# Interleaving the step-size products of one batch with the projections of the next on TensorE

## The chip, the core and the metric

The kernel runs on one core of a Trainium2 chip. The core has five engines that run their own instruction streams beside each other: TensorE (PE in the profile, with its weight loads shown as PEld), VectorE (DVE), ScalarE (ACT), GpSimd (POOL) and SyncE (SP), which here only issues DMAs. They wait for each other through counting semaphores; each engine works through its own stream in the order written. The metric is the time of one execution of the whole program in microseconds (us).

## The reference, cut to what matters

The program computes, for 8 batches of 512 tokens with 128 channels, `x + attn(layernorm(x)) + ffn(layernorm(x))`. The ffn is a mixture of 16 experts, 4 of them for each token. The attn part is a two-way Mamba block, which the change touches:

```
xz = einsum('ed,bld->bel', in_proj_w, hidden)            # 512 rows: x (256) and z (256)
for each direction (forward, backward):
    u      = silu(causal_conv(x) + conv_bias)            # 256 channels x 512 tokens
    x_dbl  = einsum('bdl,kd->bkl', u, xproj_w)           # 8 rows for the step size, 16 of B, 16 of C
    delta  = softplus(einsum('dr,brl->bdl', dtproj_w, x_dbl[:, :8]) + dt_bias)
    h      = scan(exp(delta * A), delta * B * u)         # 16 states for each channel
    y      = sum over states of h * C, + D * u, gated by silu(z)
```

"Projection" below is the product that gives x_dbl; "step-size products" are those with dtproj_w, whose output goes into delta.

## The kernel before, in words

The program has an opening (layer norm, routing, ranks), then the preparation of all 8 batches one after the other, then the main loop over the 8 batches (scans on VectorE, decays on ScalarE, products with C on GpSimd, sums and the ffn on TensorE). What a batch's preparation makes (delta, delta times u, the gate, the skip part, B and C) is stored to HBM, and the main loop reads it back.

The preparation works on whole batches: a batch has two directions (d = 0, 1) of two channel halves (h = 0, 1), 128 channels by 512 tokens each. It is pipelined over batches: while batch b goes through the step size, batch b+1 is projected, batch b+2 is convolved and batch b+3 is taken through the input projection.

On TensorE, `prepare(b)` (line 1170) issues in this order:

- the step-size products of batch b, direction 0 and then direction 1 (line 1176). Each direction has two products of 9 rows (8 rows of x_dbl and one of ones for the bias) by 128 by 512 in float32; each product shows as two matmul records, so a direction is four records. Direction d writes two PSUM banks from bank 4. It waits for `xd_sb` (ScalarE has copied x_dbl of this batch and direction) and for `delta_ready` of batch b-1 (VectorE has read the same banks).
- `project_u(b+1)` (lines 1155 to 1162): the projections of batch b+1, direction 0 and then 1, two products of 128 rows by 104 by 512 each, again four records for a direction. They write PSUM banks 2 and 3. They wait for `parts_ready` of batch b+1-1, that is for the ScalarE copy (line 915) that reads those two banks last, and for `u_ready` of their direction.
- the skip products (line 1185, eight records), `drop_part` (line 1167, which splits B and C into bfloat16 parts), `project_x(b+3)` (line 1145) and `project_z(b+3)` (line 1151).

On ScalarE, `prepare(b)` (lines 917 to 953) issues: a table load; for each direction the absolute value of the step-size products (line 923, waits for `dt_ps`) and its exponential (line 926); the logarithm of direction 0 (933); the copies of x_dbl of batch b+1, direction 0 (905 and 906, wait for `xd_ps`); the square of direction 0 (937, waits for VectorE's minimum); logarithm and square of direction 1; the x_dbl copies of direction 1; the copy of the skip products (943); the copies 910 and 887 (the latter waits for `project_x`); SiLU of batch b+2 (899); SiLU of z (892); and last the copy 915, which sets `parts_ready`.

On VectorE, `prepare(b)` (lines 1471 to 1505) issues: three of four taps of the convolution of batch b+2 (1459, 1464); the minimum of direction 0 and of direction 1 (1481, each waits for that direction's exponential, `exp_ready`); the last tap; for each direction three passes that put the softplus together (1489, 1493, 1497); and two products with u (1505).

SP stores what a batch's preparation made, in order, through the batches; after the stores of batch 6 it issues the reads of the first batch (539, 544, 547) and of the first experts' weights (558, 570, 572), then the stores of batch 7 (606), the reads of the first expert rows (561, 562) and, after the semaphore `prepared`, the rows of C (654), for which GpSimd's first product (838) waits. Beside the preparation GpSimd issues 128 scatters of token rows (804).

Of the kernel before, what the change touches and what calls it, by code (L numbers as in the profile page):

```python
# [15 lines left out]
BATCH, L = 8, 512  # L16
# [5 lines left out]
ND = 2  # L22
# [239 lines left out]
def wait(eng, semaphore, value):  # L262

    if not isinstance(value, int) or value > 0:
        eng.wait_ge(semaphore, value)
# [28 lines left out]
def build_kernel(nc, x_in, consts_in, chan_in, inw_in, xproj_in, dtw_in, outw_in,  # L294
                 route_in, b2_in, w1_in, w2_in, out):
    with ExitStack() as ctx:
# [3 lines left out]
        def sem(name):  # L300
            return ctx.enter_context(nc.semaphore(name))
# [172 lines left out]
        s = {n: sem(n) for n in names.split()}  # L474
# [624 lines left out]
        def _(pe):  # L1099
# [41 lines left out]
            def project_x(b):  # L1141
                wait(pe, s["skip_sb"], b - 2)
                wait(pe, s["z_sb"], b)
                for h in range(NH):
                    last = nc.tensor.matmul(ps[:, h, :], inw[:, h * P:(h + 1) * P], xnT[:, b * L:(b + 1) * L], start=True, stop=True)  # L1145
                last.then_inc(s["xz_ps"], 1)

            def project_z(b):
                pe.wait_ge(s["xpad_ready"], b + 1)
                for t in range(TPB):  # L1150
                    last = nc.tensor.matmul(ps[:, t // 2, t % 2 * DIN:(t % 2 + 1) * DIN], xnT[:, b * L + t * P:b * L + (t + 1) * P],
                                            inw[:, DIN:2 * DIN], start=True, stop=True)
                last.then_inc(s["z_ps"], 1)

            def project_u(b):
                wait(pe, s["parts_ready"], b)
                for d in range(ND):
                    pe.wait_ge(s["u_ready"], ND * b + d + 1)
                    for h in range(NH):
                        last = nc.tensor.matmul(ps[0:BR + NR, XD_BANK + d, :], xproj[:, d, h, :], u[b % U_RING][:, d * NH + h, :],  # L1160
                                                start=h == 0, stop=h == NH - 1)
                    last.then_inc(s["xd_ps"], 1)

            def drop_part(b, k, part, ready, written):
                for d in range(ND):
                    pe.wait_ge(s[ready], b + 1 if k else ND * b + d + 1)
                    nc.tensor.matmul(ps[0:BR, XD_BANK + d, :], drop[0:BR, k, :], part[0:BR, d, :],
                                     start=False, stop=True, skip_group_check=True).then_inc(s[written], 1)

            def prepare(b):  # L1170
                for d in range(ND):
                    pe.wait_ge(s["xd_sb"], ND * b + d + 1)
                    if b > 0:
                        pe.wait_ge(s["delta_ready"], ND * (b - 1) + d + 1)
                    for h in range(NH):
                        last = nc.tensor.matmul(ps[:, DT_BANK + d * NH + h, :], dtw[BR:BR + NR + 1, d, h * P:(h + 1) * P],  # L1176
                                                xdbl[BR:BR + NR + 1, d, :], start=True, stop=True)
                    last.then_inc(s["dt_ps"], 1)
                if b + 1 < BATCH:
                    project_u(b + 1)  # L1180

                wait(pe, s["z_sb"], min(b + 3, BATCH))
                for h in range(NH):
                    for d in range(ND):
                        last = nc.tensor.matmul(ps[:, h, :], diag[:, d * NH + h, :], u[b % U_RING][:, d * NH + h, :],
                                                start=d == 0, stop=d == ND - 1)
                last.then_inc(s["skip_ps"], 1)
                if b + 1 < BATCH:
                    drop_part(b + 1, 0, part1, "part1_ready", "rest_ps")
                if b + 3 < BATCH:  # L1190
                    project_x(b + 3)
                if b + 1 < BATCH:
                    drop_part(b + 1, 1, part2, "part2_ready", "parts_ps")
                if b + 3 < BATCH:
                    project_z(b + 3)
# [3 lines left out]
            project_x(1)  # L1199
            pe.wait_ge(s["drop_ready"], 1)  # L1200
            project_u(0)
            project_z(1)
            drop_part(0, 0, part1, "part1_ready", "rest_ps")
# [3 lines left out]
            for b in range(BATCH):  # L1207
                prepare(b)
# [480 lines left out]
```

## Time and profile before

| what | value |
| --- | --- |
| median of 3 runs | 1097.3 us |
| lowest and highest run | 1092.97 and 1101.39 us |
| span of the profiled execution | 1105.0 us |
| busy in it | PE 932.6, DVE 1030.1, ACT 940.6, POOL 909.1 us |
| preparation of batches 0 to 7 in it | from about 84 to 250 us |

For the profiled execution the page gives its span alone, and no other time of its own; the span is 7.7 us above the median of the runs. The profile's page gives busy times, the chain of work that ended last, and the costliest groups; the trace behind it answers questions on a stretch of time or a line. Times in rows are in us from the span's start unless marked ns. A granted clock (PEclk) of 1.00 is 2.4 GHz and 0.50 is 1.2 GHz.

### The profile page before, as it was taken

The numbers are of one execution on the slowest core, as the hardware profiler recorded it, in microseconds if no ns is written. First come the engines' busy times: TensorE is split into PE (matmuls) and PEld (weight loads), VectorE is DVE, ScalarE is ACT, GpSimd is POOL, SyncE is SP. The second block draws the span as 40 slices with busy tenths as digits, with TensorE's granted clock in tenths as the row PEclk, the third lists the DMA queues.
The fourth block names the chain that finished last, engine by engine and source line by source line (L and its number), as shares of the span: only waits on it lengthen the run. The fifth ranks groups of instructions, "written<-read, shape, count | busy, mean of one in ns | idle before, by whom it ended". The sixth has DMA issues, their size and how long they took to land.

```text
span 1105.0 us, 21807 instructions
## 1 busy us (share of the span) xinstructions
PE 932.6 (84%) x5794; PEld 735.3 (67%) x5866; DVE 1030.1 (93%) x1361; ACT 940.6 (85%) x1755; POOL 909.1 (82%) x567
## 2 busy tenths in 40 slices
PE   4569889955789898999998989989889989988894
PEld 2133333324678787878887877878778878877783
DVE  7789999777999999999999999999999999988897
ACT  3247999968899989999998999999989989988960
POOL 4178888863679999999999899989999999989762
PEclk9778888677999999999999999999999999998997
DMA  9945655689556767687778767776876787666668
GB/s 306 371 147 204 249 197 187 254 282 309 169 166 172 215 193 212 175 238 195 187 201 212 203 166 211 195 208 174 233 200 178 210 216 203 161 171 164 174 137 240
DMA packets 153108, 228.87 MB, mean 207 GB/s; under 512 B 36301, under 2 KB 98029, under 8 KB 147701
## 3 DMA queue, kind: packets, MB, share of 16 engines
q1 hardware_dynamic: 125844, 208.39, 58.6%
q0 software_dynamic: 27136, 19.02, 12.3%
q8 instruction: 51, 0.84, 0.3%
q14 instruction: 77, 0.62, 0.2%
HBM read 161.84 MB, written 69.64 MB: 209 GB/s over the span
## 4 chain that ended last, share of the span: by engine, by line
POOL 34%; issue 30%; ACT 14%; PE 10%; DVE 6%; DMA 3%; SPq 2%; POOLq 1%; ACTq 0%; DVEq 0%; another core or an unknown queue 0%
POOL arena L838 19%; POOL acc_d L823 14%; ACT arena L1068 3%; PE ps L1176 2%; PE ps L1160 2%; ACT arena L986 1%; DMA acc_d<-yrows,tags 1%; PE ps L1145 1%; ACT arena L1007 1%; DVE arena L1464 1%; ACT arena L937 1%; ACT arena L933 1%; ACT arena L1036 1%; PE ps L1244 1%; PE ps L1273 1%
## 5 line engine op out<-in xcount | busy, mean ns | idle before, releaser
L1568 DVE TENSOR_TENSOR_SCAN arena<-arena,ps 128x512 f32<-128x512 f32 x512 | 599.0, 1205 | 1.8 <-issue 0.8
L838 POOL TENSOR_TENSOR arena<-arena 128x1024 f32<-128x1024 f32 x246 | 527.2, 2469 | 54.6 <-DVE arena L1568 34.9
L1068 ACT ACTIVATE arena<-delta,a_neg 128x511 f32<-128x511 f32 x512 | 341.3, 728 | 2.6 <-DVE arena L1568 2.4
L823 POOL DMA_INDIRECT acc_d<-yrows,tags x160 | 252.7, 1579 | 45.2 <-issue 37.1
L1244 PE MATMUL ps<-ident,arena 128*128 128x128 f32 x2048 | 270.2, 275 | 4.6 <-DVE arena L1576 3.4
L1556 DVE TENSOR_TENSOR ps<-du,ps 128x512 f32<-128x512 f32 x352 | 233.2, 679 | 25.9 <-issue 9.5
L1244 PEld LDWEIGHTS ps<-ident,arena 128*128 128x128 f32 x2048 | 232.9, 142 | 15.1 <-DVE arena L1576 3.8
L804 POOL DMA_INDIRECT slots_d<-arena,pos x128 | 149.2, 1165 | 40.2 <-issue 35.8
L1273 PE MATMUL ps<-w,arena 128*128 128x128 f32 x1248 | 173.9, 282 | 3.4 <-ACT arena L1036 3.0
L1273 PEld LDWEIGHTS ps<-w,arena 128*128 128x128 f32 x1248 | 153.7, 192 | 12.8 <-issue 3.8
L1265 PE MATMUL ps<-rowsT,w 128*128 128x256 f32 x640 | 154.7, 385 | 7.8 <-ACT arena L1018 7.5
L986 ACT ACTIVATE arena<-arena 128x256 f32<-128x256 f32 x320 | 145.5, 511 | 0.0
L1265 PEld LDWEIGHTS ps<-rowsT,w 128*128 128x128 f32 x640 | 119.0, 193 | 26.7 <-ACT arena L1018 9.1
L1007 ACT ACTIVATE arena<-ps,w 128x256 f32<-128x256 f32 x312 | 123.8, 477 | 7.2 <-PE ps L1265 6.4
L1305 PE MATMUL ps<-ident,arena 128*128 128x128 f32 x640 | 95.0, 278 | 19.8 <-DVE arena L1568 16.0
L1305 PEld LDWEIGHTS ps<-ident,arena 128*128 128x128 f32 x640 | 74.3, 143 | 25.1 <-DVE arena L1568 18.0
L1013 ACT ACTIVATE yrows<-ps,tags 128x128 f32<-128x128 f32 x160 | 49.8, 365 | 46.7 <-PE ps L1275 21.0
L1036 ACT ACTIVATE arena<-arena 128x1024 f32<-128x1024 f32 x78 | 79.1, 1054 | 0.2
L1464 DVE SCALAR_TENSOR_TENSOR arena<-arena,chan 128x512 f32<-128x512 f32 x96 | 64.7, 742 | 0.0
L1258 PE MATMUL ps<-ident,rows 128*128 128x128 f32 x160 | 33.5, 291 | 36.6 <-ACT arena L1007 22.3
L1160 PE MATMUL ps<-arena 128*104 128x512 f32 x64 | 48.8, 934 | 5.3 <-DVE arena L1523 5.3
L1258 PEld LDWEIGHTS ps<-ident,rows 128*128 128x128 f32 x160 | 18.3, 142 | 51.9 <-ACT arena L1007 22.0
(154 smaller groups left out, 915.2 us busy)
## 6 DMA issues: line engine op xcount, KB each, us to landing
arena<-c_d SPq DMA_DIRECT2D x128, 512.0 KB
w<-w_dram SPq DMA_DIRECT2D x80, 258.0 KB
w<-w_dram SPq DMA_DIRECT2D x80, 256.0 KB
rows<-slots_d SPq DMA_DIRECT2D x80, 130.0 KB
slots_d<-delta SPq DMA_DIRECT2D x5, 2015.0 KB, 18.7
delta_d<-arena SPq DMA_DIRECT2D x8, 1024.0 KB
du_d<-delta SPq DMA_DIRECT2D x8, 1024.0 KB
delta<-delta_d SPq DMA_DIRECT2D x8, 1024.0 KB, 6.6
```

The costliest lines, as they stand in the source:

```text
L804: pool.indirect_dma_start(slots_d, bass.IndirectOffsetOnAxis(ap=pos[:, t * TOPK + k:t * TOPK + k + 1], axis=0), xn[:, t, :], None).then_in ...
L823: pool.indirect_dma_start(acc_d[j % W_RING], bass.IndirectOffsetOnAxis(ap=tags[:, j, a, 0:1].bitcast(I32), axis=0), yrows[:, j % W_RING, a ...
L838: nc.gpsimd.tensor_tensor(state[:, q % H_RING], state[:, q % H_RING], c_rows[:, r % C_RING], ALU.mult).then_inc(s["prod_done"], 1)
L986: last = nc.scalar.activation(scaled_du[scaled_slot(g, j)][:, t, :], duT[:, par, t, :], ACT.Identity, scale=bT[:, par, t, n:n + 1])
L1007: last = nc.scalar.activation(hidden[hidden_slot(b, j)][:, c, :], bank[:, f * S:(f + 1) * S], ACT.Identity, bias=w1[:, j % W_RING, FF + c: ...
L1068: nc.scalar.activation(decay[:, q % DA_RING, j, lo:lo + L - 1], delta[:, par, dh, lo:lo + L - 1], ACT.Exp, scale=a_neg[:, dh, 2 * g + j:2 ...
L1244: last = nc.tensor.matmul(y_ps[:, h, t * P:(t + 1) * P], state[:, q % H_RING, j, t * P:(t + 1) * P], ident[:, :], is_transpose=True, start ...
L1265: last = nc.tensor.matmul(bank[:, f * S:(f + 1) * S], w1[:, slot, c * P:(c + 1) * P], rowsT[:, :], start=True, stop=True)
L1273: nc.tensor.matmul(bank[:, a * P:(a + 1) * P], kept[:, c, a * P:(a + 1) * P], w2[:, slot, c, :], start=c == 0, stop=False)
L1305: last = nc.tensor.transpose(bank[:, t * P:(t + 1) * P], scaled_du[scaled_slot(g, j)][:, t, h * P:(h + 1) * P], ident[:, :])
L1556: nc.vector.tensor_tensor(b_ps[:, ROW[q, j], j, :], du[:, par, q % DH, :], b_row, ALU.mult)\
L1568: nc.vector.tensor_tensor_scan(state[:, q % H_RING, j, way], decay[:, q % DA_RING, j, way], b_ps[:, ROW[q, j], j, way], 0.0, ALU.mult, ALU ...
```

## The change

In `prepare(b)` on TensorE the projection of batch b+1 is split by direction and moved into the loop over directions. The order of issue was: step-size products of directions 0 and 1, projections of directions 0 and 1. It becomes: step-size products of direction 0, projection of direction 0, step-size products of direction 1, projection of direction 1. The wait for `parts_ready` stays ahead of the projection of direction 0, and now stands ahead of the step-size products of direction 1 too. For batch 7 no next batch is projected, and nothing changes. No instruction is added or removed, and the streams of the other engines are the same.

```diff
-            def project_u(b):
-                wait(pe, s["parts_ready"], b)
-                for d in range(ND):
+            def project_u(b, ways=range(ND)):
+                if 0 in ways:
+                    wait(pe, s["parts_ready"], b)
+                for d in ways:
                     pe.wait_ge(s["u_ready"], ND * b + d + 1)
...
                     last.then_inc(s["dt_ps"], 1)
-                if b + 1 < BATCH:
-                    project_u(b + 1)
+                    if b + 1 < BATCH:
+                        project_u(b + 1, (d,))
```

## Rows read from the trace of the kernel before

**Rows 1.** Windows over two periods; busy us (x instructions) by engine, clock, DMA.

```profile
core 0: us, PE busy (x) PEld busy (x) DVE busy (x) ACT busy (x) POOL busy (x), PEclk, DMA share, GB/s
128.30:148.90 20.60, 17.36 (x41) 7.31 (x40) 20.04 (x27) 19.32 (x22) 16.74 (x15) 0.92 0.58 214
148.90:169.50 20.60, 19.05 (x41) 7.70 (x40) 20.04 (x27) 19.32 (x22) 16.62 (x17) 0.83 0.58 211
```

**Rows 2.** Waits of ScalarE, 105 to 222 us: line, releaser, total, times, longest.

```profile
ACT arena L887 <- PE ps L1145: 7.4, 5, 2.8
ACT arena L905 <- PE ps L1160: 0.5, 1, 0.5
ACT arena L937 <- DVE du L1481: 0.3, 1, 0.3
```

**Rows 3.** Timeline of ScalarE, batches 2 and 3: start, us, line, operation.

```profile
130.47 0.99 ACT L915 CAST arena<-ps 96x1024 bf16<-96x1024 f32 x1
...
151.09 0.99 ACT L915 CAST arena<-ps 96x1024 bf16<-96x1024 f32 x1
...
155.42 1.01 ACT L923 ACTIVATE arena<-ps 128x1024 f32<-128x1024 f32 x1
...
159.40 1.15 ACT L937 ACTIVATE arena<-du,fit_bias 128x1024 f32<-128x1024 f32 x1
...
163.47 1.01 ACT L943 COPY gatedT<-ps 128x1024 f32<-128x1024 f32 x1
...
166.56 1.01 ACT L887 COPY arena<-ps 128x1024 f32<-128x1024 f32 x1 [1.16 <-PE ps L1145]
...
171.70 0.99 ACT L915 CAST arena<-ps 96x1024 bf16<-96x1024 f32 x1
```

**Rows 4.** Timeline of VectorE: the products with u of batches 2 and 3.

```profile
148.30 2.35 DVE L1505 TENSOR_TENSOR delta<-arena 128x1024 f32<-128x1024 f32 x2
...
169.44 2.41 DVE L1505 TENSOR_TENSOR delta<-arena 128x1024 f32<-128x1024 f32 x2
```

**Rows 5.** Timeline of TensorE, batches 0, 2 and 3.

```profile
101.09 3.59 PE L1145 MATMUL ps<-arena 128*128 128x512 f32 x4 [0.49 <-ACT gatedT L943]
...
128.32 3.92 PE L1176 MATMUL ps<-arena 9*128 9x512 f32 x8
132.18 5.11 PE L1160 MATMUL ps<-arena 128*104 128x512 f32 x8
...
148.94 4.06 PE L1176 MATMUL ps<-arena 9*128 9x512 f32 x8
152.93 6.67 PE L1160 MATMUL ps<-arena 128*104 128x512 f32 x8
159.43 3.60 PE L1185 MATMUL ps<-arena 128*128 128x512 f32 x8
...
164.54 1.98 PE L1145 MATMUL ps<-arena 128*128 128x512 f32 x4 [0.49 <-ACT gatedT L943]
```

**Rows 6.** Windows of TensorE alone: us, busy, granted clock, DMA.

```profile
149.00:153.00 4.00, 4.00 (x10) 0.89 0.29 107
153.00:156.00 3.00, 3.00 (x4) 0.50 1.06 405
156.00:159.40 3.40, 3.40 (x5) 0.56 0.98 388
208.20:215.60 7.40, 7.36 (x8) 0.50 0.60 227
232.00:238.40 6.40, 6.40 (x9) 0.57 1.02 342
```

**Rows 7.** Timeline, batch 6: step-size products, projection, and what waits for them.

```profile
210.21 0.99 ACT L915 CAST arena<-ps 96x1024 bf16<-96x1024 f32 x1
...
211.92 0.50 PEld L1176 LDWEIGHTS ps<-arena 9*128 9x128 f32 x2 [1.59 <-issue]
...
215.62 0.42 PEld L1160 LDWEIGHTS ps<-arena 128*104 128x104 f32 x2 [1.50 <-issue]
...
215.79 1.03 ACT L923 ACTIVATE arena<-ps 128x1024 f32<-128x1024 f32 x1 [1.17 <-PE ps L1176]
...
219.46 0.59 ACT L905 COPY arena<-ps 104x512 f32<-104x512 f32 x1 [0.51 <-PE ps L1160]
...
221.66 1.23 DVE L1489 SCALAR_TENSOR_TENSOR arena<-arena,du 128x1024 f32<-128x1024 f32 x1 [3.03 <-ACT arena L937]
```

**Rows 8.** The chain that ended last, from the preparation into the main loop.

```profile
229.26 2.36 DVE delta L1505 x2
231.63 0.66 SPq L605
232.31 0.71 SPq L606
...
252.47 0.78 SPq L606
...
258.60 4.93 DMA arena<-c_d
263.59 0.08 issue
263.69 2.56 POOL arena L838 x2
```

**Rows 9.** Timeline of GpSimd: the last scatter and the first product.

```profile
243.29 0.96 POOL L804 DMA_INDIRECT slots_d<-arena,pos  x1 [0.31 <-issue]
263.69 5.91 POOL L838 TENSOR_TENSOR arena<-arena 128x1024 f32<-128x1024 f32 x3 [19.43 <-DMA arena<-c_d]
```

## The prediction

> **What bounds the kernel now.** The windows over two periods of the preparation come first, to see who has slack. In 20.60 us VectorE is busy for 20.04 and ScalarE for 19.32, TensorE for 17.36 to 19.05 [rows 1]. Only TensorE has some, and what it makes is needed at fixed points of ScalarE's stream.
>
> ScalarE's waits are next. After the first batches it waits for one thing only that matters, the copy of `project_x` (7.4 us over 5 batches); for the step-size products it does not wait in batches 1 to 5, and for the projection of the next batch it waits once, for 0.5 us [rows 2]. Its timeline of batch 3 shows a stream without holes: the copy at line 915 starts at 151.09 and the next batch's at 171.70, a period of 20.61 [rows 3]. VectorE's period, from one product with u to the next, is 21.14 (148.30 to 169.44) [rows 4]. It runs back to back, so it falls 0.53 us behind ScalarE in each batch.
>
> The chain of waits tells how the preparation hands over to the main loop. At 229.26 VectorE multiplies batch 6 by u; then SP stores it (232.31) and issues reads and stores in one unbroken row until the C rows, whose landing starts GpSimd at 263.69 and with it the main loop [rows 8]. The last scatter began at 243.29 and GpSimd then stood still for 19.43 us [rows 9]. So a delay of batch 6 moves the main loop by as much, and the main loop itself is not touched by the change.
>
> **The change part by part.** It removes and adds no instruction, and no DMA moves. Three things are moved.
>
> *1. The projection of direction 0 goes ahead.* Its start is not set by TensorE's order alone but by `parts_ready`, the end of the copy at line 915: that starts at 130.47 and the projection at 132.18, 1.71 later [rows 3, 5]. The step-size products of both directions ran in front of this wait for nothing (128.32 to 132.24, 3.92 us [rows 5]). So TensorE waits there in the new order for about 2 us, after direction 0 alone. The projection comes no earlier. Had it come earlier, the only reader that waited for it was worth 0.5 us [rows 2].
>
> *2. The step-size products of direction 1 go behind that wait and behind four projection records.* Who waits for them: ScalarE at line 923 of direction 1; behind that stands ScalarE's whole stream, and VectorE's minimum of direction 1, with the last convolution tap and the softplus passes behind it. ScalarE wants them 4.33 us after the start of the copy at 915 (151.09 to 155.42 [rows 3]). They will be there after 1.71 us, plus four projection records, plus their own four records up to ScalarE's start.
>
> The price of those eight records hangs on TensorE's clock. At 1.2 GHz: in batch 6, the four records from 211.92 to the next group at 215.62 took 3.70, and ScalarE started at 215.79, 3.87 after the first of them [rows 7]. At 2.4 GHz: four records of `project_x` took 1.98, and ScalarE's copy of them (166.56) started 2.02 after the first (164.54) [rows 3, 5]. So the stall of ScalarE in each batch is between
> - 1.71 + 1.98 + 2.02 - 4.33 = 1.38 us, both groups at 2.4 GHz
> - 1.71 + 3.70 + 2.02 - 4.33 = 3.10 us, the projection at 1.2 GHz only
> - 1.71 + 3.70 + 3.87 - 4.33 = 4.95 us, both at 1.2 GHz.
>
> I take the third. In batch 3 the step-size products ran at nearly full clock (0.89), and the projection behind them at 0.50 and 0.56, until 159.4 [rows 6]. In batch 6, where the step-size products came in two halves with a pause between, as they will now everywhere, the whole stretch of them was at 0.50 [rows 6]. Products of 9 rows with a pause behind them were followed by 1.2 GHz in these rows, and the new order has just that ahead of the projection and again 9-row products behind it.
>
> The Trainium skill has a rule that weighs against this reading. "TensorE: Matmul & The Clock Gate", Part 1, lets the clock follow how busy the engine has recently been and knows no size of product in that. By it eight unbroken step-size records would keep the clock up, and the sum would be nearer to the first line; the trace speaks against it, since TensorE was busy for 4.00 of the 4.00 us ahead of the fall at 153.0 [rows 6].
>
> *3. Direction 1's projection and the skip products follow as before.* From line 923 of direction 1 to the skip copy are 8.05 us on ScalarE (155.42 to 163.47 [rows 3]). I cost them at nothing: four projection records (3.70) and the skip products (3.60 at full clock [rows 5]) fit in. If the clock stays at 1.2 GHz through them, the cover is gone (below).
>
> **The sum.** No batch before repays a stall: the period is ScalarE's own stream and its wait for `project_x`, both of which start from the stalled point. It becomes 20.61 + 4.95 = 25.56, over VectorE's 21.14, which then waits for the exponential of direction 1 instead.
> - Batch 0: nothing. All its waits were met long before.
> - Batches 1 to 5: 5 x 4.95 = 24.8 us. Against it stands ScalarE's wait for VectorE of 0.3 us, which vanishes [rows 2].
> - Batch 6: the copy at 915 starts at 210.21, so the projection starts at 211.92, step-size direction 1 at 215.62, ScalarE at 219.49 and not at 215.79: 3.7 us [rows 7]. Given back: VectorE's first softplus pass came 5.87 us after that (221.66), held by the late projection; without that it comes 5.13 after (159.40 + 1.15 - 155.42 [rows 3]), 0.7 less.
> - Batch 7: nothing, its TensorE order is the old one.
> - Behind it: SP's row of issues just starts later, nothing.
>
> Together 24.8 - 0.3 + 3.7 - 0.7 = 27.5; I take 26, since in batch 1 the clock falls only after the first records. Against the profiled span that is 1105.0 + 26 = 1131. That execution is 7.7 us above the median of the runs; the preparation adds the same to each, so 1097.3 + 26 = 1123.
>
> **The rivals.**
> - *Only the projection runs at 1.2 GHz.* The batch 2 projection was at full clock for its second half (5.11 us against 6.67 in batch 3 [rows 5]). Then 5 x 3.10 - 0.3 + (211.92 + 3.70 + 2.02 - 215.79 = 1.85) - 0.7 = 16 us [rows 7]: 1113.
> - *Not slower: the clock holds at 2.4 GHz.* Breaking the long stretch of 9-row products in two could keep the clock up. Then step-size direction 1 is only 1.38 us late, and the point that decides is whether the eight records take more than the 2.62 us between 1.71 and 4.33. 5 x 1.38 - 0.3 + 0.1 - 0.7 = 6 us: 1103, which a measurement of this kernel can't tell from no change (1%, 11 us). For it speaks that the clock was 0.92 and 0.83 over whole periods [rows 1]; against it, that the pause of 2 us is new. The rule of the Trainium skill named above, on the same page and section, leads here as long as that pause is too short to count as idle.
> - *No effect, or faster by the 0.5 us of wait for the projection.* It needs SP's row of issues, or the scatters, to be the bound. The scatters have 19 us in hand and SP follows the store at once [rows 8, 9], so this has little.
> - *The skip products become the bound.* At 1.2 GHz they take 6.40 [rows 6]; from the start of step-size direction 1 that is 3.70 + 3.70 + 6.40 + 0.4 = 14.2 us until the copy can start, against 3.87 + 8.05 = 11.9: 2.3 more in each batch. If `project_x` too is slow (3.59 against 1.98 [rows 5]), 1.6 more. 5 x 3.9 = 19.5 on top: 1143.
>
> **How the numbers follow.** Forecast 0.58; projection alone slow 0.18; skip products too 0.10; clock at 2.4 GHz 0.11; no effect or faster 0.03. The range of 1108 to 1134 holds the first two and the milder part of the third, and leaves out the last two. Slower by over 1%: the first three, 0.85 with a little taken off for the second case's edge; within 1%: 0.13; faster: 0.02.
>
> **What would show it.** In the changed kernel: ScalarE at line 923, second of each pair, waits for TensorE's line 1176 by 4 to 5 us in each of batches 1 to 5, and by about 5 in batch 6; its period is 25 to 26 us; VectorE waits for line 926 and its share falls to about 0.8; the step-size products of direction 1 run at 0.5; the projection starts 1.7 us after line 915, as before; SP's stores of batch 6 are issued about 26 us later, and GpSimd's first product comes at about 290. From there to the end the time is that of before. I am wrong if the second half of the step-size products runs at full clock, or if the wait for `project_x` grows beyond 1.2 us in most batches.

## The result: slower, by half of what was forecast

| | median us | runs | lowest to highest |
| --- | --- | --- | --- |
| before | 1097.11 | 4 | 1092.97 to 1101.39 |
| changed | 1109.68 | 4 | 1108.54 to 1112.99 |

The ratio is 1.0116, with a 95% interval of 1.009 to 1.0141; a second set of runs gave 1.015 (1.0119 to 1.018). So the change costs 12.6 us by the medians (9.9 to 15.5 by the interval), or 17.0 by the medians of the second set (1112.7 against 1095.7), where 26 were forecast. The direction was right and the size was off by a factor of about two.

The profiled execution of the changed kernel has a span of 1111.2 us and took 1112.99, the slowest of its four. The waits of ScalarE in batches 1 to 5, which answer to [rows 2] (line, releaser, total, times, longest):

```profile
ACT arena L887 <- PE ps L1145: 9.7, 4, 3.0
ACT arena L923 <- PE ps L1177: 7.0, 5, 2.9
```

The stall at line 923 is there in all five batches, but it is 1.4 us on average and not 4.95. And the wait for `project_x` is 2.6 to 3.0 us in three of batches 1 to 4 (batch 5 has none), where it had been 1.2 in all four; in batch 0 it was 2.8 before and is 3.0 now. ScalarE's timeline of batch 3, beside [rows 3]:

```profile
152.63 0.99 ACT L915 CAST arena<-ps 96x1024 bf16<-96x1024 f32 x1
...
157.65 1.02 ACT L923 ACTIVATE arena<-ps 128x1024 f32<-128x1024 f32 x1 [0.60 <-PE ps L1177]
...
165.72 1.02 ACT L943 COPY gatedT<-ps 128x1024 f32<-128x1024 f32 x1
...
170.23 1.01 ACT L887 COPY arena<-ps 128x1024 f32<-128x1024 f32 x1 [2.59 <-PE ps L1145]
...
175.37 0.99 ACT L915 CAST arena<-ps 96x1024 bf16<-96x1024 f32 x1
```

The period is 22.74 us (152.63 to 175.37) where it was 20.61: 0.7 at line 923 (5.02 us behind the copy at 915, and not 4.33) and 1.4 at line 887. TensorE in the same batch, beside [rows 5]:

```profile
153.68 1.97 PE L1161 MATMUL ps<-arena 128*104 128x512 f32 x4 [0.91 <-ACT arena L915]
155.57 1.98 PE L1177 MATMUL ps<-arena 9*128 9x512 f32 x4
157.48 1.97 PE L1161 MATMUL ps<-arena 128*104 128x512 f32 x4
159.29 3.60 PE L1186 MATMUL ps<-arena 128*128 128x512 f32 x8
162.72 0.38 PE L1168 MATMUL ps<-arena 96*96 96x512 bf16 x1
165.88 0.42 PE L1168 MATMUL ps<-arena 96*96 96x512 bf16 x1 [2.78 <-ACT arena L906]
166.79 3.41 PE L1145 MATMUL ps<-arena 128*128 128x512 f32 x4 [0.49 <-ACT gatedT L943]
```

Here is what I had wrong. The projection is at full clock now (1.97 for each direction, where both took 6.67 together), and so is direction 1 of the step size. TensorE is done with the skip products and the first record of `drop_part` at 163.1 and then has nothing for 2.78 us, since ScalarE has not yet made the copy that the second record needs; `project_x` behind that pause runs at 1.2 GHz, 3.41 us and not 1.98. In the kernel before, the same pause was shorter (batches 2 and 3):

```profile
143.02 0.42 PE L1167 MATMUL ps<-arena 96*96 96x512 bf16 x1 [2.08 <-ACT arena L906]
...
163.63 0.42 PE L1167 MATMUL ps<-arena 96*96 96x512 bf16 x1 [0.39 <-ACT arena L906]
```

In the other batches of the changed kernel the two go together too: the pause is 3.41 us in batch 0 and 2.78 in batches 2 and 4, with `project_x` at 3.78 or 3.79 us, and in batch 1 there is no such pause and `project_x` takes 1.99. It is not the only way to the low level: batch 0 of the kernel before paused for only 1.57 us there and had `project_x` at 3.59. The windows of TensorE in the changed kernel (us, busy, clock, DMA):

```profile
153.70:157.40 3.70, 3.70 (x8) 1.00 1.03 399
157.50:163.00 5.50, 5.50 (x14) 1.00 0.91 335
166.80:170.00 3.20, 3.20 (x4) 0.55 0.62 228
176.40:180.00 3.60, 3.58 (x4) 0.53 0.98 385
```

The clock stood at its upper level through both groups in question and the skip products, and was down at `project_x`. The last is the projection of direction 0 in the next batch, at 1.2 GHz after all, so the low level does not stay in one place.

The hand-over, which is the way from batch 6's product with u to the main loop, beside [rows 8] and [rows 9]: SP's store of batch 6 and its C rows, GpSimd's first product.

```profile
241.33 0.33 SPq L606 DMA_DIRECT2D du_d<-delta  x1
...
258.70 0.33 SPq L606 DMA_DIRECT2D du_d<-delta  x1
...
263.36 2.49 SPq L654 DMA_DIRECT2D arena<-c_d  x4
```

```profile
268.66 5.91 POOL L838 TENSOR_TENSOR arena<-arena 128x1024 f32<-128x1024 f32 x3 [30.14 <-DMA arena<-c_d]
```

From the store of batch 6 to the first product are 27.3 us (241.33 to 268.66) where they were 31.4 (232.31 to 263.69 [rows 8, 9]). So in this pair of executions the hand-over does not just start later, it gives something back; how much of that is chance is asked below.

### The profile page after: what moved, and what is told of

The parts are those of the page before. It is cut to its first block, busy times and chain, and to the rows that moved or that the text cites. A ratio compares the mean times of both kernels' runs of the same rounds, so it can differ in the third digit from the quotient of the medians.

```text
span 1111.2 us, 21879 instructions
## 1 busy us (share of the span) xinstructions
PE 942.7 (85%) x5866; PEld 737.5 (66%) x5866; DVE 1030.1 (93%) x1361; ACT 940.5 (85%) x1755; POOL 904.1 (81%) x567
## 4 chain that ended last, share of the span: by engine, by line
issue 16%; POOL 16%; ACT 16%; PE 10%; DMA 2%; DVE 1%; SPq 1%; POOLq 0%; ACTq 0%; DVEq 0%
POOL acc_d L823 8%; POOL arena L838 8%; ACT arena L1068 5%; PE ps L1274 3%; PE ps L1245 3%; ACT arena L1036 2%; ACT arena L1007 2%; ACT arena L986 2%; PE ps L1266 2%; PE ps L1306 1%; ACT yrows L1013 1%; DMA tags<-slots_d 1%; ACT L1068 1%; ACT L1036 1%; PE ps L1276 1%
## 5 line engine op out<-in xcount | busy, mean ns | idle before, releaser
L1245 PEld LDWEIGHTS ps<-ident,arena 128*128 128x128 f32 x2048 | 235.8, 143 | 15.3 <-DVE arena L1577 3.9
L804 POOL DMA_INDIRECT slots_d<-arena,pos x128 | 146.1, 1141 | 38.8 <-issue 35.0
L1306 PE MATMUL ps<-ident,arena 128*128 128x128 f32 x640 | 95.2, 280 | 16.6 <-DVE arena L1569 13.1
L1306 PEld LDWEIGHTS ps<-ident,arena 128*128 128x128 f32 x640 | 74.8, 144 | 21.9 <-DVE arena L1569 16.0
L1309 PE MATMUL ps<-parts,sel 128*128 128x512 bf16 x176 | 59.1, 391 | 10.3 <-DVE arena L1569 10.3
```

The lines of the kernel that those rows point to most:

```text
L804: pool.indirect_dma_start(slots_d, bass.IndirectOffsetOnAxis(ap=pos[:, t * TOPK + k:t * TOPK + k + 1], axis=0), xn[:, t, :], None).then_in ...
L1245: last = nc.tensor.matmul(y_ps[:, h, t * P:(t + 1) * P], state[:, q % H_RING, j, t * P:(t + 1) * P], ident[:, :], is_transpose=True, start ...
L1306: last = nc.tensor.transpose(bank[:, t * P:(t + 1) * P], scaled_du[scaled_slot(g, j)][:, t, h * P:(h + 1) * P], ident[:, :])
```

## The experiments

Each ratio is against the kernel before, timed beside that run; its medians were 1097.1 us for `changed` and 1095.7, 1096.95, 1098.1 and 1098.1 in the four later sets, and the ratio is the one on record, not the quotient of two medians. In the table, "lead" is the start of the first absolute value of batch 0, since the opening ahead of it varies by some us; the stalls at 923 are those of direction 1 in batches 0 to 6, summed from the timeline, and the waits at 887 are the five for `project_x`. The last two columns are the distance in us from the lead to the start of batch 6's product with u and to GpSimd's first product.

| kernel | ratio (95%) | median us | stalls at 923 | waits at 887 | to batch 6 | to product |
| --- | --- | --- | --- | --- | --- | --- |
| before | 1 | 1097.1 | 1.2 | 7.4 | 139.5 | 173.9 |
| before_again | 0.9995 (0.9978 to 1.0013) | 1095.3 | 0.3 | 7.3 | 140.6 | 172.8 |
| changed | 1.0116 (1.009 to 1.0141) | 1109.7 | 11.5 | 12.6 | 155.2 | 184.9 |
| change_again | 1.015 (1.0119 to 1.018) | 1112.7 | 15.3 | 11.1 | 156.9 | 186.6 |
| wait_only | 1.0003 (0.9983 to 1.0023) | 1095.3 | 1.7 | 5.8 | 140.8 | 171.3 |
| change_early_parts | 1.0069 (1.0042 to 1.0096) | 1103.5 | 6.9 | 11.9 | 150.0 | 180.1 |
| before_early_parts | 1.0005 (0.9989 to 1.0022) | 1097.1 | 0 | 5.8 | 141.0 | 172.8 |
| change_fill_gap | 1.0142 (1.0108 to 1.0177) | 1110.2 | 16.6 | 5.8 | 156.1 | 186.8 |
| change_early_fill | 1.0055 (1.0034 to 1.0077) | 1102.5 | 2.8 | 7.9 | 142.0 | 173.7 |
| change_early_fill_again | 1.0041 (1.0018 to 1.0065) | 1104.6 | 8.7 | 8.3 | 149.3 | 180.2 |
| projections_first | 1.0237 (1.021 to 1.0264) | 1123.5 | 25.1 | 14.8 | 170.2 | 201.1 |
| change_not0 | 1.0114 (1.009 to 1.0139) | 1111.3 | 10.8 | 12.5 | 155.9 | 186.0 |
| change_early_not0 | 1.0057 (1.0035 to 1.0079) | 1104.7 | 3.4 | 12.0 | 148.7 | 179.0 |
| change_three_cures | 1.0056 (1.0032 to 1.0081) | 1103.9 | 3.3 | 6.9 | 143.0 | 175.4 |

The theory after the result: the loss has two terms, the late absolute value of direction 1 and `project_x` at 1.2 GHz, and the clock sets the size of both. The rivals: that the pause alone does it, that the order does it by itself, and that the difference of the two profiles is chance. In the expectations "theory A" is this theory or the part of it that the run bears on, and "theory B" is that run's rival.

### Two second profiles

No edit.

> The kernel before, unchanged, for a second profiled execution of it. Both theories: the same time as before (1097 us). What it is to tell is how much of the first profile was its own: the stretch from the first absolute value of batch 0 to the product with u of batch 6 was 139.5 us in the first profile of the kernel before and 155.2 in that of the changed one. If that difference belongs to the change, this run shows 138 to 142 again, with ScalarE's waits for project_x at 1.2 us in four of five batches; if it is the phase of TensorE's clock that happened to be good in that one execution, it shows 145 or more.

> The changed kernel, unchanged, for a second profiled execution. Theory A (the stall comes from the wait and eight records, and the clock's level decides its size batch by batch): 1108 to 1112 us; ScalarE waits for the step-size products of direction 1 by 0.6 us in the batches in which the eight records run at 2.4 GHz, and by 2.3 to 2.9 where half of them run at 1.2 GHz, in other batches than in the first profile. Theory B (the level is fixed by the program): the same batches (1 and 4) are slow again. ScalarE's wait for project_x is about 3 us in two to four of five batches by both.

The stretch to batch 6 took 140.6 and 156.9 us, against 139.5 and 155.2 in the first profiles; `wait_only` and `before_early_parts`, which cost nothing, had 140.8 and 141.0. So the 14 to 17 us come from the change and not from chance. The stalls at 923 were 5.26 in batch 0 and 2.96, 0.60, 0.60, 0.60 and 2.25 in batches 1 to 5, and in the first profile 1.26 and 2.91, 0.60, 0.60, 2.29, 0.60. So batches 0 (its size), 4 and 5 changed places: the level is not fixed by the program, as theory A said. The time, 1112.7, is just above the 1108 to 1112 that was expected. `before_again` came out as expected, down to the waits for `project_x`: 1.2 us in four of five batches and 2.63 in batch 4, where in the first profile batch 0 had the long one (2.77).

### The wait alone

```diff
                 for d in range(ND):
+                    if d == 1 and b + 1 < BATCH:
+                        pe.wait_ge(s["parts_ready"], b + 1)
                     pe.wait_ge(s["xd_sb"], ND * b + d + 1)
```

> The order of before, but with the wait for parts_ready ahead of the step-size products of direction 1, so the pause is there and the four projection records are not between. Theory A (wait and projection records together make ScalarE late): the products of direction 1 start 1.05 us after the copy at 915 starts and are there 2.07 us later, 3.1 us against the 4.33 that ScalarE takes, so no stall at 2.4 GHz and 0.6 us at 1.2 GHz: 1097 to 1101 us. Theory B (the pause alone costs, since it lowers the clock for what follows): ScalarE's waits for project_x grow to 3 us as in the changed kernel, 1104 to 1108 us.

1.0003, nothing measurable (0.9983 to 1.0023). The wait ahead of direction 1 costs nothing without the projection in between, and the waits for `project_x` did not grow either. ScalarE over the whole preparation:

```profile
ACT arena L887 <- PE ps L1145: 5.8, 5, 1.2
ACT arena L923 <- PE ps L1178: 3.4, 3, 1.7
```

### More projection records between

```diff
-                    if b + 1 < BATCH:
-                        project_u(b + 1, (d,))
+                    if b + 1 < BATCH and d == 0:
+                        project_u(b + 1)
```

> The changed kernel with both directions of the projection ahead of the step-size products of direction 1: eight projection records stand there and not four, the wait is the same. Theory A (the records between are what makes direction 1 late): each batch from 0 to 6 loses another 1.9 us at 2.4 GHz and up to 3.7 us at 1.2 GHz on top of the changed kernel, 13 to 20 us in all: 1123 to 1132 us. Theory B (the pause and the clock set the loss, the number of records does not): 1109 to 1114 us, as the changed kernel.

1123.5 us, at the low end of theory A and far from theory B. The stalls at 923 are 2.3 or 4.0 us in batches 1 to 5 where they had been 0.6 or 2.3 to 3.0; four records more added 1.7 at 2.4 GHz (0.60 to 2.32). The waits for `project_x` grew too, to 14.8 us in all. With `wait_only` this shows what the first term needs: the wait and the projection records together.

### The late copy made early

```diff
                 if b + 3 < BATCH:
                     take_x(b + 3)
+                if b + 1 < BATCH:
+                    take_parts(b + 1)
                 if b + 2 < BATCH:
                     take_u(b + 2)
                 if b + 3 < BATCH:
                     take_z(b + 3)
-                if b + 1 < BATCH:
-                    take_parts(b + 1)
```

> The changed order on TensorE, and on ScalarE the copy that sets parts_ready is moved ahead of the SiLUs of batch b+2 and of z, by about 4 us, so the projection of direction 0 follows the step-size products of direction 0 without a pause. Theory A (the stall at the absolute value of direction 1 needs the late wait): it is gone, and with it the pause; what may be left is the wait for project_x: 1097 to 1102 us. Theory B (the interleaving itself costs, through the clock or the order of records): 1106 to 1111 us, as the changed kernel.

> Control: the order of before on TensorE, with only ScalarE's copy that sets parts_ready moved ahead of the SiLUs. In the kernel before the projection was held by TensorE's own order rather than by that copy, so by either theory 1094 to 1098 us, the time of before; if the moved copy by itself costs or brings something, it shows here, and the result of the changed kernel with it has to be read against this one.

The control is flat (1.0005). With the changed order the stalls at 923 are gone in batches 1 to 5, as theory A has it, but the time came back only by half, to 1.0069. The profile still has stalls at line 923 in batch 0 (1.4 and 5.3 us), in batch 6 (1.7) and in batch 7 (1.5 and 1.3, as in the changed kernel), and the waits for `project_x`:

```profile
ACT arena L887 <- PE ps L1145: 11.9, 5, 3.0
ACT arena L923 <- PE ps L1177: 11.1, 5, 5.3
```

1103.5 is above the 1102 that theory A allowed; I had left out that TensorE, without a pause in the middle, is done with the skip products even earlier: it pauses for 3.36 us in batches 3 and 4, where the changed kernel had 2.78, and `project_x` behind it took 3.22 and 3.78 us.

### The pause ahead of project_x filled

```diff
-                for h in range(NH):
+                for h in (0, 0, 1):
                     for d in range(ND):
                         last = nc.tensor.matmul(ps[:, h, :], diag[:, d * NH + h, :], ...
```

> The changed kernel, with the skip products of the first channel half issued twice (four records more in each batch, the same values), so that TensorE's pause of 2.8 us ahead of project_x is filled to about 1 us. Theory A (a part of the loss is project_x at 1.2 GHz after that pause): ScalarE's wait for project_x falls from about 3.0 to 1.2 us in every batch and the time by 4 to 7 us, to 1104 to 1108 us. Theory B (all of the loss is the late absolute value of direction 1): no better, or 1 to 2 us worse by the added records, 1111 to 1114 us.

> Both cures on the changed order: the copy that sets parts_ready ahead of the SiLUs, and the skip products of the first half issued twice. Theory A (two terms, the late absolute value and project_x after a pause, make all of the loss): 1095 to 1099 us, no different from before but for up to 5 us in batch 0, whose products still stand behind the projection. Theory B (something else is in it): 1102 us or more.

> The same kernel as change_early_fill for a second profiled execution; 1100 to 1104 us again. If its usual loss of 5 us is batch 0, the profile shows a stall of about 5 us at the absolute value of direction 1 in batch 0; if it is project_x or the skip copy, waits of 2 to 3 us in three or more batches.

With the changed order alone the filled pause did to `project_x` what it should, and the time did not move: 1.0142, between the 1.0116 and 1.015 of the changed kernel, and 1110.2 us where theory A had 1104 to 1108. Its waits of ScalarE over the whole preparation:

```profile
ACT arena L923 <- PE ps L1177: 18.4, 9, 3.4
ACT arena L887 <- PE ps L1145: 5.8, 5, 1.2
ACT gatedT L943 <- PE ps L1186: 3.7, 3, 1.5
```

The 1.2 GHz had moved. TensorE in batch 2 of this kernel:

```profile
126.47 2.70 PE L1161 MATMUL ps<-arena 128*104 128x512 f32 x4 [1.22 <-ACT arena L915]
129.11 3.78 PE L1177 MATMUL ps<-arena 9*128 9x512 f32 x4
132.81 3.74 PE L1161 MATMUL ps<-arena 128*104 128x512 f32 x4
...
143.49 1.98 PE L1145 MATMUL ps<-arena 128*128 128x512 f32 x4 [0.67 <-ACT gatedT L943]
```

`project_x` takes 1.98, and direction 1 of the step size 3.78. So theory A was right on the term and wrong on its worth: the stalls at 923 rose to 16.6 us in batches 0 to 6 (11.5 and 15.3 without the fill) while the waits for `project_x` fell from 12.6 and 11.1 to 5.8. Each of batches 1 to 5 now had a stall of 2.0 to 3.4 us at 923, and the low level had not gone but moved.

With the wait gone too, `change_early_fill` gave 1.0055 and, in the second set, 1.0041, against 1.0069. The intervals overlap, so it is not shown that the fill helps there. And 1102.5 us is what the rival had (1102 or more) and not the 1095 to 1099 of theory A: something beyond the two terms was left. The profiled execution of the first set was the fastest of its six (1099.96 us) and that of the second the slowest of its twelve (1109.8). The second one lost 5.26 us in batch 0 and 3.40 in batch 6 at line 923, and 2.8 in all at the skip copy; the first one 1.26, 1.53 and nothing before batch 7. So the same kernel shows a good and a bad case of the clock.

### Batch 0 in its old order

```diff
-                    if b + 1 < BATCH:
+                    if 0 < b < BATCH - 1:
                         project_u(b + 1, (d,))
+                if b == 0:
+                    project_u(b + 1)
```

> The changed order from batch 1 on, batch 0 in the order of before. By the two profiles of the changed kernel batch 0 stalls ScalarE by 1.3 us in one and by 5.3 us in the other, where the prediction had nothing. If that stall is passed on, the time is 1 to 5 us below the changed kernel, 1106 to 1110 us; if VectorE's own backlog hides it, 1109 to 1113 us.

> The changed order from batch 1 on with ScalarE's copy that sets parts_ready moved ahead of the SiLUs. The copy moved alone gave 1103.5 us with the changed order in all batches, and its profile had a stall of 5.3 us in batch 0 and none in batches 1 to 5. Theory A (the rest of its loss is batch 0 and project_x): 1098 to 1102 us. Theory B (batch 0 is hidden): 1102 to 1105 us.

Neither moved clear of noise: 1.0114 for 1.0116 and 1.015, and 1.0057 for 1.0069. Both times (1111.3 and 1104.7) lie where the stall of batch 0 was expected to be hidden (1109 to 1113 and 1102 to 1105); the intervals leave room for some us, and no more can be said. The stall in batch 0 is gone from the profile, and batches 2 and 3 had 2.25 and 2.24 in it where the changed kernel's two profiles had 0.60 in both.

> The changed order from batch 1 on, ScalarE's copy that sets parts_ready ahead of the SiLUs, and the skip products of the first half issued twice. Theory A (late wait, batch 0 and project_x at 1.2 GHz make the whole loss): ScalarE waits for project_x by 1.2 us in every batch, and the time is 1096 to 1100 us. Theory B (the filled pause only moves the 1.2 GHz stretch to other records, as it did in the changed kernel with the pause filled): 1101 to 1105 us, with stalls at the absolute value or at the skip copy in its place.

All three together: 1.0056, not below 1.004. Theory A expected 1096 to 1100 us and 1103.9 came out, so it is not the whole. In the profile four of five waits for `project_x` are at 1.17 and batches 0 to 5 have no stall at line 923; the stretch to batch 6 is 143.0 us, 2.4 above that of `before_again`. Of its waits the stall of batch 6 (3.3) stands out; the 6.9 at line 974 is behind the last batch's preparation, and `before_again` has 7.3 there:

```profile
ACT arena L887 <- PE ps L1145: 6.9, 5, 2.3
ACT arena L974 <- PE ps L1220: 6.9, 1, 6.9
ACT arena L923 <- PE ps L1177: 3.5, 2, 3.3
ACT gatedT L943 <- PE ps L1188: 2.2, 2, 1.4
```

The executions of this kernel spread from 1098.6 to 1108.5 us, and the profiled one (1103.8) is at their median (1103.9), so its profile has to show the usual loss. It does so in two parts. GpSimd's first product comes 175.4 us after the lead, 2.6 later than in `before_again`. From there to the end it takes another 841.9 us, against 839.2 in `before_again` (and 841.3, 839.1 and 837.9 in `before`, `wait_only` and `before_early_parts`). So about half of what is left of the loss against `before_again` lies behind the preparation, in a stretch whose own spread is as large; whether the change has a part in it is not shown.

### How much of a delay reaches the end

```diff
+                    for k in range(8 if b == 6 and d == 0 else 0):
+                        nc.vector.tensor_tensor(du_p[:, way], pos_part[:, way], u[b % U_RING][:, way], ALU.mult).then_inc(s["v_chain"], 1)
+                        dve.wait_ge(s["v_chain"], start + (KC - 1) * DH * BATCH + k + 1)
```

> The kernel before, with the first product with u of batch 6 done eight times more on VectorE (about 9.9 us), so that batch 6 is handed over that much later and nothing else changes. As in the prediction (SP's row of issues just starts later): the first product of GpSimd and the end come 9.9 us later, 1105.5 us. Rival (SP's row is partly a queue of transfers that empties in the meantime): it gives back 2 to 5 us, 1100 to 1104 us.

1104.85 against 1096.95 us, ratio 1.0071 (1.0051 to 1.0091): 7.9 us, and 5.6 to 10.0 by the interval. What went in was 10.1 us by the trace (the added products start at 227.28 and batch 6's own at 237.35), where 9.9 had been planned. So some 2 us were given back, at the low end of the rival, but the upper end of the interval is all but the whole delay. The time itself, 1104.85, is nearer to the 1105.5 of the prediction's reading than to the rival's 1100 to 1104, since the kernel before took 1.3 us more beside this run than the expectation assumed.

The profiles say more. GpSimd's first product came 180.6 us after the lead, 7.8 later than in `before_again`. From the start of batch 6's own products with u to VectorE's first scan there were 24.3 us here, and 23.9 to 24.3 in the five other profiles in which batch 6 came over 10 us late (`changed`, `change_again`, `change_fill_gap`, `projections_first`, `change_not0`); with no delay of batch 6 there were 29.1, 27.0, 26.3 and 26.7 (`before`, `before_again`, `wait_only`, `before_early_parts`). Where it came 8 to 10 us late there were 24.9 to 26.2. So about 2 us or more are given back before the first scan when batch 6 is 10 us late. To GpSimd's first product the two groups overlap (29.5 to 30.9 against 30.6 to 34.4), so how much is given back up to there is uncertain.

### Taking the hand-over apart

```diff
             for b in range(BATCH - 1):
+                if b == BATCH - 2:
+                    read_ahead()
+                    read_weights()
                 store_prepared(b)
-            read_ahead()
-            read_weights()
             store_prepared(BATCH - 1)
-            read_first()
             sp.wait_ge(s["prepared"], 1)
...
                 read_c(0, r)
+            read_first()
+            for k in range(2 * NH):
+                read_late(0, 0, k)
```

(`read_ahead` no longer issues the gate and skip reads, which are the last two lines.)

> A version meant to be faster: the order of before on all engines but SP. SP issues the reads of the first batch and of the first weights ahead of the stores of batch 6, and behind the stores of batch 7 first the C rows, then the first expert rows and the gate and skip parts of the first batch. In the second profile of the kernel before the reads of the first batch land at 241.0 us, 13 us after their issue and 16 us after batch 6's product with u starts, and the first scan starts at 251.6, 26 us after it. If these reads hold the first scan, it now comes 4 to 5 us earlier and the time is 1090 to 1093 us; if the reads ahead of the stores delay batch 7's preparation by as much, 1095 to 1098 us.

1098.4 against 1098.1: no gain, and not for the reason that I gave. The first scan did come early, 162.1 us after the lead where `before_again` had 167.6, but from it to the end it took 848.8 us and not 844.4, since VectorE soon stopped:

```profile
243.95 2.33 DVE L1568 TENSOR_TENSOR_SCAN arena<-arena,ps 128x512 f32<-128x512 f32 x2
246.19 0.68 DVE L1556 TENSOR_TENSOR ps<-du,ps 128x512 f32<-128x512 f32 x1
246.77 2.32 DVE L1568 TENSOR_TENSOR_SCAN arena<-arena,ps 128x512 f32<-128x512 f32 x2
255.44 1.29 DVE L1556 TENSOR_TENSOR ps<-du,ps 128x512 f32<-128x512 f32 x2 [6.35 <-PE ps L1308]
```

TensorE stood at its transposes of the first expert rows, in front of the B rows that VectorE needed:

```profile
254.29 0.69 PE L1258 MATMUL ps<-ident,rows 128*128 128x128 f32 x2 [12.90 <-DMA tags<-slots_d]
```

The next version keeps everything but reads the expert rows ahead of the C rows, as before (`read_first()` goes back in front of the wait for `prepared`).

> The kernel before with SP's reads of the first batch and weights ahead of the stores of batch 6, as in before_reads_early, but the first expert rows are read ahead of the C rows again. There the first scan came 5 us earlier and then VectorE stood still for 6.4 us until TensorE had the expert rows, which landed at 254 us. With the rows issued right after batch 7's stores they land at about 249, so this stall goes, and the time is 1091 to 1094 us; if C rows or rows take longer beside the stores, 1095 to 1099 us as before.

1092.8 against 1098.1 us, ratio 0.9949 (0.9926 to 0.9972): faster than both kernels, and in the expected range. The first scan is as early as in the version above (161.8 us after the lead), and from it to the end are 844.1 us again. TensorE has the rows at 246.54, and the B rows no longer come late:

```profile
246.54 0.69 PE L1258 MATMUL ps<-ident,rows 128*128 128x128 f32 x2 [5.62 <-DMA tags<-slots_d]
```

```profile
243.46 2.32 DVE L1568 TENSOR_TENSOR_SCAN arena<-arena,ps 128x512 f32<-128x512 f32 x2
245.70 0.67 DVE L1556 TENSOR_TENSOR ps<-du,ps 128x512 f32<-128x512 f32 x1
246.28 2.32 DVE L1568 TENSOR_TENSOR_SCAN arena<-arena,ps 128x512 f32<-128x512 f32 x2
248.51 1.27 DVE L1556 TENSOR_TENSOR ps<-du,ps 128x512 f32<-128x512 f32 x2
```

## Why the prediction was half right

**Right: the direction and the path.** The stall sits where the prediction put it, at line 923 of direction 1, ScalarE's stream and VectorE's minimum behind it stand still with it, and most of the delay of batch 6 reaches the main loop. `wait_only` and `projections_first` show that it takes the wait and the records together. "I cost them at nothing", of the direction 1 projection and the skip products, held too (157.65 to 165.72 is 8.07 us, against 8.05 before). That the measured time lies inside the stated range is in part luck: the term below was far too large, and a term that the prediction did not have made up for some of it.

**Wrong: the term of 4.95 us in each batch.** This is the step that failed: the stall of ScalarE with both groups at 1.2 GHz, five times in the sum. It measured 2.91, 0.60, 0.60, 2.29 and 0.60 us in batches 1 to 5, 7.0 in all where 24.8 were forecast; in batch 6 the changed order added 2.0 (3.20 against 1.17) where 3.7 were forecast. Two of its parts failed.
- The 1.71 us ahead of the projection were read as the reach of `parts_ready`. They were TensorE's own queue: the step-size products lasted until 132.24 and the projection began at 132.18 [rows 5]. With only half of them in front, the projection starts 1.05 us after the copy (152.63 to 153.68). Worth 0.66 in each batch; by the rows of batch 3 the case at 2.4 GHz is 1.05 + 1.89 + 2.08 - 4.33 = 0.69, half of the 1.38 that the prediction gave for it.
- The two groups at 1.2 GHz. I took the clock from rows in which an unbroken row of eight 9-row records stood ahead (batch 3) or in which the engine had been low before (batch 6). Broken up by records of 128 rows, as in the changed kernel, it held in three of batches 1 to 5 in each profile (stalls of 0.60) and fell in the other two (2.25 to 2.96). So the rival "the clock holds at 2.4 GHz", to which I gave 0.11, had this part nearly right, and the first of the two signs of being wrong, the second half of the step-size products at full clock, came true in four of these five batches of the first profile (1.98 us; 3.78 in batch 1). It is also where the rule of the Trainium skill ("TensorE: Matmul & The Clock Gate", Part 1) pointed, by which the clock follows how busy the engine has recently been; the rule does not explain the kernel before, where TensorE had been busy for 4.00 of 4.00 us ahead of the fall [rows 6].

**Missing: project_x.** The prediction let ScalarE's wait for it stay at 1.2 us, and named its growth as the other sign of being wrong. It grew by 5.2 us in all (7.4 to 12.6): in three of the four batches in which it had been 1.16 it was 2.6 to 3.0. This is the price of the faster projection: TensorE finished early, paused for 2.78 us, and the next records were at 1.2 GHz, with ScalarE right behind them. That the pause has to do with it is shown by `change_fill_gap`, where all five waits were back at 1.2; that removing it gains time is not, since the low level turned up elsewhere.

**Missing: batch 0.** Forecast at nothing, since its waits "were met long before". Its second absolute value waited for 1.26 us in one execution and 5.26 in the other. By `change_not0` and `change_early_not0` it is worth some us at most, and nothing could be measured of it.

**Off by a little: the hand-over.** "SP's row of issues just starts later, nothing" was some 2 us off in `before_delay6`, where 10.1 us went in and 7.9 came out (with an interval up to 10.0), and 2.5 to 4.7 in the changed kernel's first profile (to batch 6: 155.2 against 139.5 to 140.6; to the first product: 184.9 against 172.8 to 173.9). About 2 us on the way to the first scan are in all six profiles with batch 6 over 10 us late. Where SP's row of issues gains them was not taken apart.

The sum with what was measured, from the first profiles: stalls at 923 in batches 0 to 6 11.5 - 1.2 = 10.3, `project_x` 5.2, together 15.5 against 15.7 for the stretch to batch 6. Less 15.7 - 11.0 = 4.7 given back in the hand-over of these two executions leaves 11.0, and the medians differ by 12.6. The first profile of the kernel before had the longer hand-over of its two; with `before_again` in its place it is 14.6 less 2.5, or 12.1.

What stays open: with all three cures the changed order still loses 0.6% (0.3 to 0.8). Its profile, a median execution, shows 2.6 us of that ahead of GpSimd's first product, with a stall in batch 6 among them, and about as much behind it, where no cause was looked for. What sets TensorE's level at a given place was not found either.

## What to carry to other kernels

A product moved behind another engine's late copy costs only what the copy and the records in front of it add beyond the time its reader takes to arrive: 0.6 us a batch here with TensorE at 2.4 GHz, 2 to 3 where it was at 1.2, and nothing when no record stood between. Work that TensorE gets done sooner may only move its pause to a worse place, as here ahead of `project_x`; look at what runs behind the new pause, at which clock, and who waits for it. A profile shows one execution: before a stall is put down to the program, look at where that execution stands among the others and take a second one. And a hand-over between two stages is a chain of its own with several gates in a row: taking one away (the first scan 5 us earlier) brought nothing until the next, the expert rows, was kept from moving behind it.

## What the runs showed of the hardware

- Eight records of 9 rows in an unbroken row were followed by the low level in batch 3 of the kernel before: busy for 4.00 of 4.00 us, then at 0.50 [rows 6]. The same records alternating in fours with records of 128 rows ran at 1.00 together with them in batch 3 of the changed kernel (8 records in 3.70 us). It did not always hold: in batch 2 of `change_fill_gap` the same alternation was at 0.50 (129.2 to 136.4), so neither the rows nor the order alone settles the level.
- The level is not a property of the program: two executions of the same kernel had `project_x` at 1.2 GHz in batches 0, 2, 3, 4 and in batches 2, 3, 4, and the four step-size records of direction 1 in batch 0 took 1.98 us in one and 3.78 in the other.
- The order of a few reads on one queue moved a small one by much. With the first tags (2 KB) and expert rows (130 KB) issued behind the four C rows of 512 KB, the tags at 246.55, TensorE waited for them until 254.29, 7.7 us after the issue; with both ahead of the C rows, the tags at 244.23, it waited until 246.54, 2.3 us after.
